# Pass two's offset convolution: nine taps in three column groups of the PE array, added up by a selecting matmul at the turn

## The chip, the cores and the metric

The kernel runs on one core of one Trainium2 chip. The time is the device time of one execution in microseconds. The engines are TensorE (PE, with its weight loads as PEld), VectorE (DVE), ScalarE (ACT), GpSimd (POOL), which here only issues gathers, and SyncE (SP), which issues plain DMAs.

## What is computed

The input is 32 images of 96 channels and 48 x 48 pixels. Two layers run one after the other. The first is a state space mixer and a quantised feed-forward net; the second, which the change touches, is a deformable convolution and another feed-forward net:

```python
offset = _conv(x, offset_w, offset_b)           # 3x3, 96 -> 18 channels
mask = jax.nn.sigmoid(_conv(x, mask_w, mask_b)) # 3x3, 96 -> 9 channels
for k in range(K * K):
    i, j = (k // K, k % K)
    py = base_y[None, :, None] + i * DIL + offset[:, 2 * k]
    px = base_x[None, None, :] + j * DIL + offset[:, 2 * k + 1]
    samp = _bilinear(x, py, px) * mask[:, k][:, None]
    out = out + jnp.einsum('bchw,oc->bohw', samp, weight[:, :, i, j])
```

The two small convolutions are done as one, with 27 output channels and nine taps: the offset convolution.

## The kernel before

Pass one (up to 13.4 ms of the trace) does the scans of the first layer and is not touched. Pass two takes the images in a software pipeline: one call of `pass_two`, a stage, finishes image d (called D) while it prepares image c (called C). There are 33 stages: the first has only C, the last only D, and 31 have both. Between two stages stand barriers and the clearing of the semaphores.

An image is cut into six chunks of 384 pixels (CH), and a chunk into three tiles of 128. A stage runs seven periods p = 0 to 6 of twelve steps u = 0 to 11. Each engine has its program written out over these steps, and the order of the code is the order of the work:

- C's half, chunk c = p: the out projection (L1487, u = 1), its first feed-forward net (L1441, L1448, L1458, L1465), the norm that gives `xflat` and `xn`, the turn of `xflat` (L1497) and the rows `prow`, which SP stores to the corner table (L1381). Then comes the offset convolution of chunk q (L1516). For q = 0 to 3 it stands in period q + 2, steps 6 to 8; for q = 4 in period 6, steps 2 to 4; for q = 5 in period 6, steps 7 to 9. Its step `stage` does taps 3·stage to 3·stage + 2, all into partitions 0 to 26 of PSUM bank BM. One step later ACT adds the bias and writes `offc` (L1630), and one more step later PE turns `offc` by three transposes (L1531) and ACT splits the result into `offs` and `sig` (L1636, L1637).
- When all of C's chunks are through, DVE works out the positions and weights of all samples (`positions`, L1347 to L1366), which the gathers of the next stage need.
- D's half: POOL issues 162 indirect gathers (L1404), nine for each of 18 tiles t, into a ring G of four tiles. DVE multiplies a tile by its weights in two halves (L1680), PE turns the 36 blocks (L1420, 16 + 16 + 4), ACT copies them to `cols_t` (L1569), and once a chunk PE convolves (L1434, step 3 of the next period). Tile 3p + u // 4 is multiplied in period p at steps where u % 4 is 0 or 1, and turned one tile later. Then come the norm of chunk e (L1441 at step 6, L1448 at step 7, DVE's L1690 at step 8) and the second feed-forward net (L1458 at steps 9 and 10, L1465 at step 0 of the next period).
- SP loads the inputs of the next C after C's last rows are stored (L1388 to L1390) and stores D's output when its last chunk is done (L1394).

Of one engine's program everything waits behind a waiting instruction. All matmuls named here but L1458 and L1465 (fp8) are fp32.

Of the kernel before, what the change touches and what calls it, by code (L numbers as in the profile page):

```python
# [17 lines left out]
CH = 8 * W  # L18
# [16 lines left out]
def shape_constants():  # L35

    c = {}
    c["ident"] = np.eye(P, dtype=np.float32)
    c["centring"] = (np.eye(C) - 1.0 / C).astype(np.float32)
    c["mean"] = np.full((C, C), 1.0 / C, np.float32)  # L40
    c["ones"] = np.ones((P, P), np.float32)
    j, i = np.meshgrid(np.arange(P), np.arange(P), indexing="ij")
    c["before"] = (j < i).astype(np.float32)
    r = np.arange(C)
    state = np.repeat(np.arange(N).reshape(NG, NG), GS, axis=1)
    c["pick"] = (r[:, None, None] % (2 * N) == state[None]).astype(np.float32).reshape(C, NG * P)
    c["sel"] = (np.arange(P)[:, None, None] % GS + GS * np.arange(CG)[None, :, None] == r[None, None, :]).astype(
        np.float32).reshape(P, CG * C)
    c["shifts"] = np.concatenate([(r[:, None] == r[None, :] + k - 2).astype(np.float32) for k in range(5)], axis=1)
    px = np.arange(P)[:, None, None] + P * np.arange(NT)[None, :, None]  # L50
    tap = np.arange(TAPS)[None, None, :]
    c["base_y"] = (px // W - 1 + tap // 3).astype(np.float32).reshape(P, NT * TAPS)
    c["base_x"] = (px % W - 1 + tap % 3).astype(np.float32).reshape(P, NT * TAPS)
    c["border"] = np.ones((1, PH, PW), np.float32)
    c["border"][:, 0] = c["border"][:, -1] = 0
    c["border"][:, :, 0] = c["border"][:, :, -1] = 0
    c["border"] = c["border"].reshape(1, PH * PW)
    return c
# [11 lines left out]
def build_program(nc, I, out, B=IMAGES):  # L70

    with ExitStack() as top:
# [56 lines left out]
        off_b = cols[0:3 * TAPS, 50:51]  # L129
# [206 lines left out]
        with ExitStack() as loop:  # L336
            M = pass_two_memory(sbt, loop)
            w_def = sbt(loop, "w_def", [C, TAPS, C])
            w_off = sbt(loop, "w_off", [C, TAPS, 3 * TAPS])
# [11 lines left out]
            with ExitStack() as ctx:  # L351
                Z = sems(top, "z_set", "z_done")
                zero_rows = sbt(ctx, "zero_rows", [PH, CORNERS * C])
                with nc.Block() as block:
                    @block.vector
                    def _(dve):
                        dve.memset(zero_rows[:], 0.0).then_inc(Z["z_set"], 1)
                        dve.memset(M["xn"][:, 0:PH:PH - 1, :], 0.0)
                        dve.memset(M["xn"][:, 1:PH - 1, 0:PW:PW - 1], 0.0)

                    @block.sync
                    def _(sp):
                        sp.wait_ge(Z["z_set"], 1)
                        for table in tables:
# [5 lines left out]
                        sp.dma_start(flat(w_off), I["w_off"]).then_inc(Z["z_done"], 16)  # L370
                        sp.wait_ge(Z["z_done"], 16 * (2 * PH + 4))
# [4 lines left out]
                           w_off=w_off, off_b=off_b, w_def=w_def)  # L376
# [898 lines left out]
def pass_two_memory(sbt, ctx):  # L1275
# [4 lines left out]
        offc=b("offc", [3 * TAPS, CH]), prow=b("prow", [PT, 2, ROWT, C]), offs=b("offs", [P, NT, 3 * TAPS]),  # L1280
# [10 lines left out]
def pass_two(nc, ps, S, M, Wt, dram, parity, d_image, c_image, load):  # L1291
# [76 lines left out]
    with nc.Block() as block:  # L1368
# [42 lines left out]
        def _(pe):  # L1411
# [57 lines left out]
            for p, u in places:  # L1469
# [36 lines left out]
                if q is not None and stage < 3:  # L1506
# [8 lines left out]
                    for k in range(3 * stage, 3 * stage + 3):  # L1515
                        m = pe.matmul(ps[0:3 * TAPS, BM, 0:CH], Wt["w_off"][:, k, :],  # L1516
                                      M["xn"][:, 8 * q + k // 3:8 * q + k // 3 + 8, k % 3:k % 3 + W],
                                      start=(k == 0), stop=(k == TAPS - 1))
                    if stage == 2:
                        m.then_inc(S["p_off"], 1)  # L1520
                if q is not None and stage == 4:
# [8 lines left out]
                    for r in range(TILES):  # L1530
                        m = pe.transpose(ps[:, BN, 3 * TAPS * r:3 * TAPS * (r + 1)], M["offc"][:, r * P:(r + 1) * P],  # L1531
                                         ident[0:3 * TAPS, 0:3 * TAPS])
# [26 lines left out]
        def _(act):  # L1559
# [42 lines left out]
            for p, u in places:  # L1602
# [25 lines left out]
                if q is not None and stage == 3:  # L1628
                    act.wait_ge(S["p_off"], q + 1)
                    act.activation(M["offc"][:], ps[0:3 * TAPS, BM, 0:CH], ACT.Identity,  # L1630
                                   bias=Wt["off_b"]).then_inc(S["p_offs"], 1)
# [172 lines left out]
```

## Time and profile before

| | us |
|---|---|
| median of 3 runs | 22115.79 |
| lowest and highest | 22111.92 to 22125.49 |
| the profiled execution | 22081.76 |
| its span, first to last instruction | 22079.9 |
| mean granted TensorE clock over the span | 0.832 |

The profile is of one execution. Times of rows are microseconds from the start of the span, durations of one instruction are nanoseconds. A matmul's recorded duration holds its way through the array, so matmuls in a row overlap in the records: what one of them takes of the engine's time is the distance between their starts. A row of the timeline can hold several instructions of one line: "x6" are six.

### The profile page before, as it was taken

The page shows a single profiled execution, that of the slowest core. Times are in us where ns is not written, and L with a number is a line of the kernel's source. Part 1 is how long each engine was busy: PE and PEld are TensorE (multiplying, and loading weights), DVE is VectorE, ACT ScalarE, POOL GpSimd, SP SyncE. Part 2 cuts the span into 40 slices and gives each one's busy share as a digit, 9 for nine tenths or more (in the row PEclk, how much of TensorE's full clock was granted, in tenths as well). Part 3 has the DMA queues.
Part 4 walks back from the last instruction along what each step waited for, and adds up shares of the span by engine and source line. Part 5 has one row for each costly group of instructions (what it writes and reads, how often), then busy time and mean ns, then how long its engine had stood idle before and what let it go on. Part 6 is the DMA issues. An engine that isn't in the chain of part 4 may idle for free. (4 is left out here: it accounts for less than half of the span.)

```text
span 22079.9 us, 218895 instructions
## 1 busy us (share of the span) xinstructions
PE 15826.8 (72%) x70927; PEld 8399.6 (38%) x70927; DVE 13815.1 (63%) x14097; ACT 8761.1 (40%) x15494; POOL 11403.5 (52%) x9476
## 2 busy tenths in 40 slices
PE   6677677676676676676676665777777777777777
PEld 3233233233333333333333332444444444444444
DVE  5778778778777787777787782444444444444443
ACT  3344343343443443443443432333333333333332
POOL 3454454454454444444454453555555555555555
PEclk8788788788787787787787787988898888989898
DMA  2222222232222322322322223555555555555554
GB/s 56 71 78 73 73 77 70 76 77 68 77 77 67 78 75 68 79 73 69 79 74 69 77 78 98 148 145 147 146 149 147 148 145 146 149 147 148 146 145 133
DMA packets 1287149, 2235.23 MB, mean 101 GB/s; under 512 B 710836, under 2 KB 754216, under 8 KB 1270504
## 3 DMA queue, kind: packets, MB, share of 16 engines
q1 hardware_dynamic: 874248, 1086.64, 19.1%
q0 software_dynamic: 368640, 1076.24, 17.2%
q10 hardware_dynamic: 43008, 56.65, 0.9%
q8 instruction: 663, 10.86, 0.2%
q14 instruction: 590, 4.83, 0.1%
HBM read 1493.57 MB, written 271.92 MB: 80 GB/s over the span
## 5 line engine op out<-in xcount | busy, mean ns | idle before, releaser
L1250 POOL TENSOR_TENSOR hc<-h,crep 128x768 f32<-128x768 f32 x2304 | 4172.2, 1812 | 5950.1 <-DVE h L1029 3900.9
L1404 POOL DMA_INDIRECT G<-corners,idx x5184 | 4929.6, 951 | 3831.8 <-issue 2494.3
L646 PE MATMUL ps<-hc,sel 128*96 128x512 f32 (+1 forms) x9216 | 4080.7, 572 | 541.7 <-POOL hc L1250 337.3
L1680 DVE TENSOR_TENSOR G<-G,ps 128x1536 f32<-128x1536 f32 (+1 forms) x1152 | 2235.4, 1946 | 1890.0 <-DMA G<-corners,idx 1889.5
L1029 DVE TENSOR_TENSOR_SCAN h<-decay,carry,ps 128x768 f32<-128x768 f32 x1536 | 2774.9, 1807 | 79.0 <-ACT decay L841 19.6
L1420 PE MATMUL ps<-ident,G 128*96 128x128 f32 x20736 | 2716.7, 285 | 38.4 <-DVE G L1680 38.4
L1013 DVE TENSOR_TENSOR ps<-dxr,ps 128x768 f32<-128x768 f32 x2304 | 2180.7, 946 | 862.2 <-PE ps L635 833.5
L1420 PEld LDWEIGHTS ps<-ident,G 128*96 128x96 f32 x20736 | 2473.2, 133 | 390.3 <-issue 296.0
L646 PEld LDWEIGHTS ps<-hc,sel 128*96 128x96 f32 x9216 | 1600.1, 189 | 2543.5 <-issue 1920.2
L635 PE MATMUL ps<-bq,pick 96*128 96x512 bf16 (+1 forms) x4608 | 1298.9, 368 | 1654.0 <-DVE h L1029 1592.3
L841 ACT ACTIVATE decay<-dtr,a_neg 128x768 f32<-128x768 f32 x2304 | 2125.6, 928 | 780.8 <-DVE h L1029 710.1
L849 ACT ACTIVATE carry<-h 128x1 f32<-128x1 f32 x1536 | 308.9, 201 | 3833.5 <-DVE h L1029 3829.1
L715 PE MATMUL ps<-xcp,w_local 96*96 96x384 f32 x3456 | 1424.7, 533 | 252.8 <-ACT local_c L907 252.0
L1029 DVE TENSOR_TENSOR_SCAN h<-decay,ps 128x768 f32<-128x768 f32 x768 | 1340.2, 1745 | 21.7
L1516 PE MATMUL ps<-xn,w_off 96*27 96x384 f32 x3456 | 1288.7, 515 | 10.1 <-ACT xn L1614 10.1
L1569 ACT ACTIVATE cols_t<-ps 96x512 f32<-96x512 f32 (+1 forms) x1728 | 827.1, 481 | 1157.5 <-PE ps L1420 1157.1
L635 PEld LDWEIGHTS ps<-bq,pick 96*128 96x128 bf16 x4608 | 363.3, 101 | 2422.2 <-DVE h L1029 1749.4
L1434 PE MATMUL ps<-cols_t,w_def 96*96 96x384 f32 x3456 | 1156.3, 489 | 142.4 <-ACT prow L1620 140.0
L674 PE MATMUL ps<-xnp,w_conv 97*96 97x384 f32 x3456 | 1180.8, 486 | 42.7 <-ACT eout L932 39.2
L1575 ACT ACTIVATE sq<-ps 96x384 f32<-96x384 f32 x576 | 280.1, 486 | 2302.5 <-PE ps L1441 2299.7
L1690 DVE TENSOR_TENSOR xq<-ps,rs 96x384 fp8e5<-96x384 f32 x384 | 212.0, 552 | 1453.9 <-ACT rs L1583 1453.7
L715 PEld LDWEIGHTS ps<-xcp,w_local 96*96 96x96 f32 x3456 | 612.8, 184 | 722.8 <-ACT local_c L907 324.6
(214 smaller groups left out, 21501.1 us busy)
## 6 DMA issues: line engine op xcount, KB each, us to landing
crep<-c_rows SPq DMA_DIRECT2D x3072, 96.0 KB, 2.3
dtr<-rel SPq DMA_DIRECT2D x2304, 96.0 KB, 2.2
dxr<-mag SPq DMA_DIRECT2D x2304, 96.0 KB, 2.2
corners<-prow SPq DMA_DIRECT2D x1536, 72.0 KB
G<-corners,idx POOLq DMA_INDIRECT x5184
x_in<-in_x SPq DMA_DIRECT2D x32, 864.0 KB
local_all<-local_c ACTq DMA_DIRECT2D x192, 144.0 KB, 1.9
unit<-sorted_rows SPq DMA_DIRECT2D x32, 864.0 KB, 6.8
```

The costliest lines, as they stand in the source:

```text
L635: m = pe.matmul(wide(bank_of(("step", s)), P)[:, a:b], Wt["pick"][:, ng, :], bq[:, q % 2, a:b], start=True, stop=True)
L646: m = pe.matmul(wide(BY, C)[:, a:b], Wt["sel"][:, cg, :], hc[:, v % HC, a:b], start=(v % ROUND == 0), stop=(v % ROUND == ROUND - 1))
L674: m = pe.matmul(ps[0:C, BS + c % 2, 0:CH], Wt["w_conv"][:, t, :], xn[0:C + 1, 8 * c + t // 3:8 * c + t // 3 + 8, t % 3:t % 3 + W], start=( ...
L715: m = pe.matmul(ps[0:C, BV, 0:CH], Wt["w_local"][:, t, :], xpad[:, 8 * c + t // 3:8 * c + t // 3 + 8, t % 3:t % 3 + W], start=(t == 0), st ...
L841: act.activation(decay[:, s % 3, :], dtr[:, q % 2, cg, :], ACT.Exp, scale=Wt["a_neg"][:, direction(q)[0], ng, cg:cg + 1]).then_inc(S["s_de ...
L1013: dve.tensor_tensor(drive, dxr[:, q % 2, cg, :], drive, ALU.mult).then_inc(S["s_drive"], 1)
L1029: dve.tensor_tensor_scan(along(h[:, v % 3, :], k), along(decay[:, v % 3, :], k), along(wide(bank_of(("step", v)), P), k), first, ALU.mult, ...
L1250: pool.tensor_tensor(hc[:, s % HC, :], h[:, s % 3, :], crep[:, g % CRING, :], ALU.mult).then_inc(S["s_weighted"], 1)
L1404: pool.indirect_dma_start(M["G"][:, t % GRING, k, :], None, table_d, bass.IndirectOffsetOnAxis(M["idx"][:, t, k:k + 1], 0)).then_inc(S[f"p ...
L1420: m = pe.matmul(ps[0:C, BT + n % 2, (k % 4) * P:(k % 4 + 1) * P], M["G"][:, v % GRING, k, q * C:(q + 1) * C], ident[:], is_transpose=True, ...
L1516: m = pe.matmul(ps[0:3 * TAPS, BM, 0:CH], Wt["w_off"][:, k, :], M["xn"][:, 8 * q + k // 3:8 * q + k // 3 + 8, k % 3:k % 3 + W], start=(k = ...
L1680: dve.tensor_tensor(g, g, w.to_broadcast([P, (k1 - k0) * CORNERS, C]), ALU.mult).then_inc(S["p_prod"], 1)
```

## The change

The array is split by columns. The nine taps go to three column groups of 32 columns, one for each row i of the 3 x 3 taps; the group i writes its sum over its three taps to partitions 32·i to 32·i + 31 of the same bank. Step `stage` of the convolution now does the taps 3·i + stage of all three groups, one after the other. The three partial sums are not added there: the copy to `offc` takes all 96 partitions (the bias on the first group only), and the turn is now an ordinary matmul with `offc` as the stationary operand and a 96 x 27 matrix `sel_off` of zeros and ones as the moving one, which picks channel o from the three groups and so adds them. The weights `w_off` are padded from 27 to 32 columns, with zeros set by DVE before pass two, and three small loads join that setup.

```diff
@@ constants
+    c["sel_off"] = (r[:, None] % GS == np.arange(3 * TAPS)[None, :]).astype(np.float32)
@@ setup of pass two
-            w_off = sbt(loop, "w_off", [C, TAPS, 3 * TAPS])
+            w_off = sbt(loop, "w_off", [C, TAPS, GS])
+            off_bias = sbt(loop, "off_bias", [C, 1])
+            sel_off = sbt(loop, "sel_off", [C, 3 * TAPS])
...
+                        dve.memset(w_off[:], 0.0).then_inc(Z["z_set"], 1)
+                        dve.memset(off_bias[:], 0.0).then_inc(Z["z_set"], 1)
...
-                        sp.dma_start(flat(w_off), I["w_off"]).then_inc(Z["z_done"], 16)
+                        sp.dma_start(w_off[:, :, 0:3 * TAPS],
+                                     I["w_off"].rearrange("c (k o) -> c k o", o=3 * TAPS)).then_inc(Z["z_done"], 16)
+                        sp.dma_start(off_bias[0:3 * TAPS], I["cols"][0:3 * TAPS, 50:51],
+                                     allow_slow_non_contiguous=True).then_inc(Z["z_done"], 16)
+                        sp.dma_start(sel_off[:], I["sel_off"]).then_inc(Z["z_done"], 16)
@@ pass_two_memory
-        offc=b("offc", [3 * TAPS, CH]), prow=b("prow", [PT, 2, ROWT, C]), offs=b("offs", [P, NT, 3 * TAPS]),
+        offc=b("offc", [C, CH]), prow=b("prow", [PT, 2, ROWT, C]), offs=b("offs", [P, NT, 3 * TAPS]),
@@ pass_two, tensor
-                    for k in range(3 * stage, 3 * stage + 3):
-                        m = pe.matmul(ps[0:3 * TAPS, BM, 0:CH], Wt["w_off"][:, k, :],
-                                      M["xn"][:, 8 * q + k // 3:8 * q + k // 3 + 8, k % 3:k % 3 + W],
-                                      start=(k == 0), stop=(k == TAPS - 1))
+                    for i in range(3):
+                        m = pe.matmul(ps[GS * i:GS * (i + 1), BM, 0:CH], Wt["w_off"][:, 3 * i + stage, :],
+                                      M["xn"][:, 8 * q + i:8 * q + i + 8, stage:stage + W],
+                                      start=(stage == 0), stop=(stage == 2))
...
-                        m = pe.transpose(ps[:, BN, 3 * TAPS * r:3 * TAPS * (r + 1)], M["offc"][:, r * P:(r + 1) * P],
-                                         ident[0:3 * TAPS, 0:3 * TAPS])
+                        m = pe.matmul(ps[:, BN, 3 * TAPS * r:3 * TAPS * (r + 1)], M["offc"][:, r * P:(r + 1) * P],
+                                      Wt["sel_off"][:], start=True, stop=True)
@@ pass_two, scalar
-                    act.activation(M["offc"][:], ps[0:3 * TAPS, BM, 0:CH], ACT.Identity,
-                                   bias=Wt["off_b"]).then_inc(S["p_offs"], 1)
+                    act.activation(M["offc"][:], ps[0:C, BM, 0:CH], ACT.Identity,
+                                   bias=Wt["off_bias"][:]).then_inc(S["p_offs"], 1)
```

The places in the engines' programs stay. This is PE's program from the last turn of samples to the end of a stage, before:

```order
L1516 MATMUL ps<-xn,w_off 27x384 x3
L1434 MATMUL ps<-cols_t,w_def 96x384 x9
L1516 MATMUL ps<-xn,w_off 27x384 x6
L1531 MATMUL ps<-ident,offc 128x27 x3
L1441 MATMUL ps<-x,centring 96x384
```

And the same place in the changed kernel, whose lines are eight further down:

```order
L1524 MATMUL ps<-xn,w_off 32x384 x3
L1442 MATMUL ps<-cols_t,w_def 96x384 x9
L1524 MATMUL ps<-xn,w_off 32x384 x6
L1539 MATMUL ps<-sel_off,offc 128x27 x3
L1449 MATMUL ps<-x,centring 96x384
```

No instruction moved past another. The column groups, which these rows don't show, are in the partitions that the convolution writes.

## Rows read from the trace of the kernel before

**Rows 1.** The page's parts 1 and 2: busy shares; 40 slices of the span

```profile
PE 15826.8 (72%) x70927; PEld 8399.6 (38%) x70927; DVE 13815.1 (63%) x14097; ACT 8761.1 (40%) x15494; POOL 11403.5 (52%) x9476
PE   6677677676676676676676665777777777777777
PEclk8788788788787787787787787988898888989898
```

**Rows 2.** Timeline of POOL (start us, duration us, gathers, idle before): starts and last gathers of stages

```profile
13566.73 0.94 POOL L1404 DMA_INDIRECT G<-corners,idx  x1 [285.24 <-POOLq L160]
13768.74 0.95 POOL L1404 DMA_INDIRECT G<-corners,idx  x1 [0.30 <-issue]
...
15372.85 1.05 POOL L1404 DMA_INDIRECT G<-corners,idx  x1 [0.30 <-issue]
15431.16 0.94 POOL L1404 DMA_INDIRECT G<-corners,idx  x1 [57.26 <-POOLq L160]
...
21840.62 0.94 POOL L1404 DMA_INDIRECT G<-corners,idx  x1 [59.71 <-POOLq L160]
```

**Rows 3.** Timeline of PE: projections of two periods in a row, and the tail's begin

```profile
15321.48 0.81 PE L1487 MATMUL ps<-mix,wg 96*96 96x384 f32 x2
15356.45 0.81 PE L1487 MATMUL ps<-mix,wg 96*96 96x384 f32 x2
15371.11 2.12 PE L1516 MATMUL ps<-xn,w_off 96*27 96x384 f32 x6
15373.16 0.89 PE L1441 MATMUL ps<-x,centring 96*96 96x384 f32 x2
15384.84 0.81 PE L1441 MATMUL ps<-x,centring 96*96 96x384 f32 x2
15394.61 6.05 PE L1434 MATMUL ps<-cols_t,w_def 96*96 96x384 f32 x18
15400.59 4.05 PE L1516 MATMUL ps<-xn,w_off 96*27 96x384 f32 x12
15405.31 0.36 PE L1531 MATMUL ps<-ident,offc 27*128 27x27 f32 x3 [0.66 <-ACT offc L1630]
15406.10 0.86 PE L1441 MATMUL ps<-x,centring 96*96 96x384 f32 x2 [0.43 <-issue]
15406.89 2.12 PE L1516 MATMUL ps<-xn,w_off 96*27 96x384 f32 x6
15408.94 0.89 PE L1448 MATMUL ps<-sq,mean 96*96 96x384 f32 x2
15409.76 4.05 PE L1516 MATMUL ps<-xn,w_off 96*27 96x384 f32 x12
```

**Rows 4.** Timeline of DVE in the same stage, and tile 17 of the first stage

```profile
15366.41 1.75 DVE L1680 TENSOR_TENSOR G<-G,ps 128x1536 f32<-128x1536 f32 x1 [6.07 <-DMA G<-corners,idx]
15378.58 1.74 DVE L1680 TENSOR_TENSOR G<-G,ps 128x1536 f32<-128x1536 f32 x1
13784.05 1.74 DVE L1680 TENSOR_TENSOR G<-G,ps 128x1536 f32<-128x1536 f32 x1
```

**Rows 5.** Timeline of PEld: weight loads around the offset convolution

```profile
15064.78 0.16 PEld L1441 LDWEIGHTS ps<-x_t,centring 96*96 96x96 f32 x1 [0.16 <-issue]
...
15400.59 0.13 PEld L1516 LDWEIGHTS ps<-xn,w_off 96*27 96x27 f32 x2 [0.57 <-issue]
15400.93 0.10 PEld L1516 LDWEIGHTS ps<-xn,w_off 96*27 96x27 f32 x1 [0.22 <-issue]
15401.26 0.10 PEld L1516 LDWEIGHTS ps<-xn,w_off 96*27 96x27 f32 x1 [0.22 <-issue]
```

**Rows 6.** All instructions of the turn L1531: durations ns min/median/max

```profile
L1531 PEld LDWEIGHTS ps<-ident,offc x576: 132/136/139, 13456.6 to 21824.6; 27*128 27x128 f32 x192
```

**Rows 7.** Timeline of ACT in the tail: square after norm 3, and the chain's inverse

```profile
15407.00 0.49 ACT L1575 ACTIVATE sq<-ps 96x384 f32<-96x384 f32 x1 [0.99 <-PE ps L1441]
15410.47 0.52 ACT L1583 ACTIVATE rs<-rs 96x384 f32<-96x384 f32 x1
```

More of the change, by code:

```diff
@@ L128, in build_program @@
         local_w = cols[:, 40:49]
-        off_b = cols[0:3 * TAPS, 50:51]
         def clear(own, dma_sems):
@@ L362, in _ @@
                     def _(sp):
-                        sp.wait_ge(Z["z_set"], 1)
+                        sp.wait_ge(Z["z_set"], 3)
                         for table in tables:
@@ L369, in _ @@
                         sp.dma_start(flat(w_def), I["w_def"]).then_inc(Z["z_done"], 16)
-                        sp.dma_start(flat(w_off), I["w_off"]).then_inc(Z["z_done"], 16)
-                        sp.wait_ge(Z["z_done"], 16 * (2 * PH + 4))
+                        sp.dma_start(w_off[:, :, 0:3 * TAPS],
[3 more added lines that the diff above has]
+                        sp.dma_start(sel_off[:], I["sel_off"]).then_inc(Z["z_done"], 16)
+                        sp.wait_ge(Z["z_done"], 16 * (2 * PH + 6))
                 nc.all_engine_barrier()
@@ L375, in build_program @@
                            bn_scale=bn_scale, bn_shift=bn_shift, col=col, w1q=w1q, w2q=w2q, b1q=b1q, b2q=b2q,
-                           w_off=w_off, off_b=off_b, w_def=w_def)
+                           w_off=w_off, off_bias=off_bias, sel_off=sel_off, w_def=w_def)
             dram = dict(x=I["x"], local=local_dram, mamba=mamba_dram, tables=tables, out=out)
```

## The prediction

> **What bounds the kernel now.** The page's busy shares and slices come first [rows 1]. Pass two is the last 15 or 16 of the 40 slices, where PE stands at 7 tenths and its clock mostly at 8 and 9 tenths of full speed. That looks like a PE bound, with a convolution of 3456 matmul instructions worth cutting. The second view corrects this: the timeline of POOL. A stage's 162 gathers follow one another without a pause, 202.01 us from the first to the last in the first such stage (13566.73 to 13768.74) and 201.69 in the shown middle one, which is 1.25 us for each [rows 2]. Only 31 gaps between stages interrupt POOL. From the first gather of all to the first gather of the last stage are 21840.62 - 13566.73 = 8273.9 us in 31 stages, 266.9 each. So a stage with both halves costs 202.2 us of gathers that nothing on PE can shorten, and 64.7 us from the last gather to the next stage's first. Only these 64.7 can shrink, 2006 us in all.
>
> Third view, PE against POOL. Two projections of neighbouring periods lie 34.97 us apart [rows 3], while 27 gathers take 33.75. PE is the slower one by 1.2 us a period, so it falls behind and pays for it after the last gather. DVE's rows show how far [rows 4]: tile 16 was waited for (6.07 us idle, released by the DMA at 15366.41), so tile 17 could start nine gathers or 11.25 us later, at 15377.66, which is 4.8 us after the last gather. It started at 15378.58, 5.7 us after it. In the first stage it started 15.3 us after (13784.05 against 13768.74). Over the 31 stages, of which these two are near the ends, this distance is 5.6 to 15.7 us, 9.2 in the mean. The last chunk's convolution (L1434) starts 21.8 us after the last gather in the shown stage and 25.4 in the mean.
>
> Then comes the tail: convolution, norm 3, variance, feed-forward, positions, barriers. In the shown stage it takes 15431.16 - 15394.61 = 36.6 us, in the mean of 31 stages 39.3, and 25.4 + 39.3 = 64.7. PE has two offset convolutions in it, between steps of that very chain [rows 3].
>
> **What one step of the convolution costs.** Three taps are "x6": every fp32 matmul is two instructions in a row, each with its weight load. A call from L1516 to L1441 takes 15373.16 - 15371.11 = 2.05 us. Inside a call the loads lie 0.32 us apart and last 0.10, so PE is bound by the stream of the moving operand [rows 5]. Six times 0.32 is 1.94, and 0.11 is left at the edges. There the next line's load isn't pulled ahead: the load at 15400.59 comes with its matmul, after 0.57 us of idle, whereas 15064.78 comes a full slot before its own [rows 5]. The 27-column matmul already runs in another division of the array than its neighbours. That toll is paid now and stays.
>
> **What column groups do to it.** No row shows two groups at work together, so the saving is bounded. Call r the saving of one call of six, R that of twelve in a row (tail, 15400.59).
>
> - Upper end: all three groups stream together, and a call is two slots instead of six. r = 4 x 0.32 = 1.29, R = 2.58.
> - Lower end: no overlap, r = 0, or less than that if each change of group costs an edge (the rival below).
> - What I take: the two instructions of one matmul follow each other in the same group, so the second must wait for the first, and what starts in order behind it waits too. Second half of A goes with first half of B, second half of B with first of C. A call is four slots, r = 2 x 0.32 = 0.65, and twelve are seven, R = 1.61. If the load of a new group (0.10) can only begin when the matmul ahead has started, two of these come on top: r = 0.44, R = 1.09. I take the middle, r = 0.54 and R = 1.35, because the loads in [rows 5] start with the matmul ahead, while a group that this matmul doesn't use might be loaded sooner.
>
> The page "TensorE: Matmul & The Clock Gate" of the Trainium skill (Part 3) says that matmuls in different tiles overlap but start and end strictly in program order, which is the in-order start assumed here. The same part gives 2.38 times for three column tiles of 512 columns; by that a call would take 2.05 / 2.38 = 0.86 us, near the 0.76 of the first rival below.
>
> **The turn.** Three transposes become three ordinary fp32 matmuls, so six instructions, and each loads 128 columns (0.136 us, [rows 6]). The nearest rows bound it: three transposes take 0.36 now, and three more loads at 0.06 to 0.14 add 0.18 to 0.42. I take 0.4. The copy to `offc` is 384 elements per partition as before, on 96 partitions instead of 27; this costs nothing on an engine that works all partitions at once (0.57 us on 27, 0.52 for the 96-partition copy L1583 of the same width [rows 7]). The setup (two memsets, three loads) happens once, some us beside about a hundred row loads: nothing.
>
> **The sum for a stage with both halves.** First, PE's lag. Periods 2 to 5 have one convolution each: 4 x (3 x 0.54 - 0.4) = 4.9 us. The call at step 2 of period 6, ahead of L1434, adds 0.54, so 5.4. But the gathers set a floor. DVE can't multiply tile 17 before 4.8 us after the last gather, then comes the residual behind it (0.9), which L1441 (15384.84) waits for: 4.8 + 1.7 + 0.9 = 7.4 instead of 12.0 us after the last gather, so in the shown stage at most 4.6 + 0.54 are won. Stages with more lag get all 5.4. Mean of 31: 5.3.
>
> Second, the tail. Twelve instructions stand before the turn that norm 3 waits behind: 1.35 - 0.4. The six before L1448 at 15408.94: the square is ready at 15407.00 + 0.49, so up to 1.4 of r can be had: 0.54. The twelve before the feed-forward (15409.76): the inverse is ready at 15410.99 and DVE's multiply at 15411.6, PE at 15413.7, so up to 2.1: 1.35. The last turn has idle time of PE beside it. Sum 2.84.
>
> Together 8.1 us, times 31 = 252. The first stage has no gathers and is all chain: six convolutions of 18 instructions each save some 2 us, 12. That is 264 of 22081.8 in the profiled execution. This execution is 34 us under the median of the runs, so the saving is taken off the median: 22115.8 - 264 = 21852, rounded to **21850**.
>
> **The rivals.**
>
> *All three groups at once* (r = 1.29, R = 2.58). For: the array's columns are separate. Against: the pairs in one group. PE would save 4 x 3.5 = 14 us before the tail, and nearly every stage would run into the gathers' floor: convolution 16.0 us after the last gather instead of 25.4, so 9.4. Tail: 2.58 - 0.4 + 1.29 + 2.1 = 5.6. Together 15.0 x 31 = 465, and 21 in the first stage: **21630**.
>
> *No overlap.* The groups run one after the other, and the turns alone are added: 4 x 0.4 + 0.4 = 2.0 us a stage, 31 stages and 2 more: 64 at most, 30 with 0.18 for a turn: **22150 to 22180**. For it: no row shows overlap. The change then doesn't do what it says.
>
> *A toll at each change of group* is the case on the other side. If the array treats a new group as it treats the edge between L1516 and its neighbours, the load comes late and about 0.1 us is lost. Each call has two changes, twelve instructions five, and nothing overlaps. Periods 2 to 5: 4 x (6 x 0.1 + 0.4) = 4.0; the tail 14 x 0.1 + 0.4 = 1.8; 5.8 x 31 + 7 = 187: **22300**. With both sides of the edge counted at each change (0.11 before, 0.16 at the first matmul after, 0.89 against 0.81 in [rows 3]) it is 22500. It decides from the point where the tolls of a call exceed the overlap. Against: all nine taps are in the same division of the array.
>
> *PE gets faster but its clock falls.* The slices of the clock show 8 and 9 tenths [rows 1]; PE with more idle time could be granted 1.2 instead of 2.4 GHz more often. A slow spell doubles every slot. Eight us a stage would have to be eaten; within 0.2% of no change.
>
> **How the numbers follow.** Pairwise overlap 0.50, all three at once 0.15, no overlap 0.14, a toll 0.14, the clock 0.07. The toll, 22300 and above, is left out of the range, which spans the others with the bounds of the turn: 21620 to 22190. The likeliest case alone spans r from 0.44 to 0.65: 21800 to 21920. A measurement of this kernel can tell about 0.2%, 44 us, from no change. Faster by more than that: pairwise and all three, 0.65. Slower: toll, and half of no overlap, 0.21. Within: 0.14.
>
> **What would show it.** In the changed profile the call of six should take 1.4 to 1.6 us from its start to the next line's, not 2.05 (0.8 is the first rival, 2.05 the second, more the third); the call of twelve 3.2 to 3.7 from L1524 to the copy's release, less than 4.05; the recorded matmuls of two groups should start closer than 0.32. POOL's gathers must still take 202 us a stage. The gap between stages should shrink from 64.7 to 56.6, and tile 17 should be multiplied about 5 us after the last gather in most stages. The forecast is wrong if the groups don't overlap, if the stages' lag comes from spells of slow clock and not from PE's work, or if POOL begins to wait for PE.

## The result

| | us |
|---|---|
| before, median of 4 runs beside it | 22113.85 (22106.08 to 22125.49) |
| after, median of 4 runs | 21616.36 (21604.64 to 21625.43) |
| ratio | 0.9776, 95% interval 0.9763 to 0.9788 |
| the profiled execution of after, its span | 21612.28, 21610.5 |
| forecast | 21850, range 21620 to 22190 |

The changed kernel is 2.2% faster. The direction was right, the gain was nearly twice the forecast, and the time lies 4 us under the range. The first rival, all three groups at once, gave 21630.

One thing is needed to read the experiments. Eleven of the eighteen kernels ran on chips on which the kernel before takes 23,960 to 24,000 us. Its spans of pass two look different there (last section). Each ratio is against runs of the kernel before on the same chip, and the two settings are kept apart below.

### The profile page after: what moved, and what is told of

Read it like the earlier page. It is cut to its first block and busy times, and to the rows that moved or that the text cites. A ratio compares the mean times of both kernels' runs of the same rounds, so it can differ in the third digit from the quotient of the medians.

```text
span 21610.5 us, 220051 instructions
## 1 busy us (share of the span) xinstructions
PE 15250.9 (71%) x71503; PEld 8297.3 (38%) x71503; DVE 13802.1 (64%) x14099; ACT 8777.7 (41%) x15494; POOL 11400.7 (53%) x9476
## 3 DMA queue, kind: packets, MB, share of 16 engines
q0 software_dynamic: 368640, 1076.24, 17.6%
## 5 line engine op out<-in xcount | busy, mean ns | idle before, releaser
L1412 POOL DMA_INDIRECT G<-corners,idx x5184 | 4925.0, 950 | 3357.5 <-issue 2263.5
L1688 DVE TENSOR_TENSOR G<-G,ps 128x1536 f32<-128x1536 f32 (+1 forms) x1152 | 2237.2, 1947 | 2343.1 <-DMA G<-corners,idx 2343.1
L1442 PE MATMUL ps<-cols_t,w_def 96*96 96x384 f32 x3456 | 1156.3, 489 | 141.5 <-ACT prow L1628 139.0
L1118 DVE TENSOR_SCALAR cmp<-sim,dist 128x128 bf16<-128x128 f32 (+8 forms) x576 | 854.1, 1483 | 6.3 <-ACT sim L908 3.6
L1442 PEld LDWEIGHTS ps<-cols_t,w_def 96*96 96x96 f32 x3456 | 547.7, 163 | 686.9 <-issue 489.9
```

The lines of the kernel that those rows point to most:

```text
L1412: pool.indirect_dma_start(M["G"][:, t % GRING, k, :], None, table_d, bass.IndirectOffsetOnAxis(M["idx"][:, t, k:k + 1], 0)).then_inc(S[f"p ...
L1442: m = pe.matmul(ps[0:C, BN, 0:CH], Wt["w_def"][:, k, :], M["cols"][:, e % 2, k, :], start=(k == 0), stop=(k == TAPS - 1))
L1688: dve.tensor_tensor(g, g, w.to_broadcast([P, (k1 - k0) * CORNERS, C]), ALU.mult).then_inc(S["p_prod"], 1)
```

## The profile of the changed kernel

Lines are eight further down than before: L1524 is the offset convolution, L1539 its turn, L1412 the gather, L1688 the multiply, L1442 the convolution of samples. In twogroups, groupcall and aab the offset convolution is L1525, in normfirst its turn is L1545.

First the page's second part: PE's busy share, and the granted clock in 40 slices (answers to [rows 1]).

```profile
PE   6677677667667767767767764777777777777776
PEclk8788788778778878878878876888888888888888
```

But for the last slice, PE is as busy in pass two as before, in tenths. Part of that can come from the clock. Added up from the clock intervals after 13500 us, PE was at 1.2 GHz for 1910 of 8580 us before and for 2093 of 8110 us after.

POOL's timeline (answers to [rows 2]): the first gather of all, one stage's first and last gather, the next stage's first, and the first of the last stage.

```profile
13559.70 0.94 POOL L1412 DMA_INDIRECT G<-corners,idx  x1 [269.29 <-POOLq L160]
...
15071.18 0.94 POOL L1412 DMA_INDIRECT G<-corners,idx  x1 [51.99 <-issue]
...
15273.85 0.94 POOL L1412 DMA_INDIRECT G<-corners,idx  x1 [0.30 <-issue]
15321.38 0.94 POOL L1412 DMA_INDIRECT G<-corners,idx  x1 [46.59 <-POOLq L160]
...
21370.28 0.94 POOL L1412 DMA_INDIRECT G<-corners,idx  x1 [46.91 <-POOLq L160]
```

The gathers of a stage still take 202.7 us. The gain is in the gap behind them, 47.5 us here and 49.9 in the mean of 31, where it was 64.7. Over 31 stages a stage takes (21370.28 - 13559.70) / 31 = 251.95 us instead of 266.9. That is 14.95 x 31 = 463 us. The spans of the two profiled executions differ by 469 us, and the 7 us more lie ahead of the first gather (although pass one ended 9 us later in this execution, so the first stage gained some 16). The other 28 of the 498 us between the medians are no gain of a place in the kernel: the profiled execution before was 32 us under its median, the one after 4 us.

PE's timeline in the tail of that stage (answers to [rows 3]):

```profile
15289.26 0.85 PE L1524 MATMUL ps<-xn,w_off 96*32 96x384 f32 x6 [0.33 <-ACT xn L1622]
15290.03 6.05 PE L1442 MATMUL ps<-cols_t,w_def 96*96 96x384 f32 x18
15296.01 1.49 PE L1524 MATMUL ps<-xn,w_off 96*32 96x384 f32 x12
15298.19 0.85 PE L1539 MATMUL ps<-sel_off,offc 96*128 96x27 f32 x6 [0.69 <-ACT offc L1638]
15299.48 0.86 PE L1449 MATMUL ps<-x,centring 96*96 96x384 f32 x2 [0.43 <-issue]
15300.26 0.85 PE L1524 MATMUL ps<-xn,w_off 96*32 96x384 f32 x6
15301.04 0.89 PE L1456 MATMUL ps<-sq,mean 96*96 96x384 f32 x2
15301.85 1.49 PE L1524 MATMUL ps<-xn,w_off 96*32 96x384 f32 x12
15303.74 0.50 PE L1466 MATMUL ps<-xq,w1q 96*128 96x384 fp8e5 x2 [0.39 <-DVE xq L1698]
```

A call is 15290.03 - 15289.26 = 0.77 us instead of 2.05, twelve instructions are a row of 1.49 instead of 4.05. The weight loads agree (answers to [rows 5]; columns as there):

```profile
15296.01 0.15 PEld L1524 LDWEIGHTS ps<-xn,w_off 96*32 96x32 f32 x6 [0.57 <-issue]
15296.36 0.12 PEld L1524 LDWEIGHTS ps<-xn,w_off 96*32 96x32 f32 x3 [0.20 <-issue]
15296.68 0.12 PEld L1524 LDWEIGHTS ps<-xn,w_off 96*32 96x32 f32 x3 [0.20 <-issue]
```

Where before one load followed each 0.32 us, three stand in one row per slot. The toll of the line's edge (0.57 us idle of PEld) has stayed.

Last, DVE's tile 17 of the same stage (answers to [rows 4]), 2.96 us after the last gather's start at 15273.85:

```profile
15276.81 1.75 DVE L1688 TENSOR_TENSOR G<-G,ps 128x1536 f32<-128x1536 f32 x1 [1.94 <-DMA G<-corners,idx]
```

It waits for the DMA. In all 31 stages it starts 2.95 to 3.26 us after the last gather, 3.05 in the mean (before 9.2), and in 29 of them the profile names the DMA as what released it. The list of waits of 14000 to 20000 us says the same of all tiles, before first and after second (us in total, times, longest):

```profile
DVE G L1680 <- DMA G<-corners,idx: 1284.6, 235, 12.3
```

```profile
DVE G L1688 <- DMA G<-corners,idx: 1726.8, 384, 12.4
```

## The experiments

The question after the result was why three groups overlap fully, though the two halves of a float32 matmul follow each other in one group. The theory: a waiting second half doesn't hold up what stands behind it. PE starts a later instruction of another group. The rival: the gain isn't from overlap but from something that came with the change (padded weights, the wider copy, setup). A second question was whether the stage's time follows PE's by the path sum.

**onegroup**, all nine taps in one group again, with everything else of the change kept:

```diff
-                    for i in range(3):
-                        m = pe.matmul(ps[GS * i:GS * (i + 1), BM, 0:CH], Wt["w_off"][:, 3 * i + stage, :],
...
+                    for k in range(3 * stage, 3 * stage + 3):
+                        m = pe.matmul(ps[0:GS, BM, 0:CH], Wt["w_off"][:, k, :],
...
```

The lines left out take the taps in their old order and let `sel_off` read the first group alone.

> The changed kernel with all nine taps in column group 0 (32 columns, in the old order of the taps); copy, turn and setup stay changed. Theory (the whole gain is the overlap of the groups): a call of six takes 2.05 us again, and what is left is the dearer turn. The changed kernel's turn takes 0.69 us from its start to the next line's, against 0.30 before, so 0.39 x 5 = 2.0 us a stage on PE's path, x 31 = 60: about 22175 us, 1.0028 of before. Rival A (part of the gain comes from the copy, the padding or the turn): under 22070. Rival B (the turn is hidden in PE's waits for ACT): 22115, as before.

> The one-group kernel once more, beside the two above on the same chip: where the kernel before takes 22114, 22175 (the turns' 2.0 us a stage); where it takes 24000, 24120, as in its first run. If the clock is what differs between the two settings, its share of 1.2 GHz is that of the kernel before within 0.02.

> Theory (PE's time is what the gap follows, and only a different column group lets PE start a later instruction): all nine taps in one group give calls of 2.05 us again and leave only the longer turn, so 0 to 2 us a stage more than before, ratio 1.000 to 1.003. Where POOL's gathers take 202 us a stage this should be read in the gap: 64.7 to 66.7 us. Rival (the padded weights, the copy of 96 partitions or the setup brought the gain): 0.978, the gap 50 us.

Where before takes 23,960 to 24,000: 1.0054 (1.0037 to 1.0071) and 1.0005 (0.9995 to 1.0014), 23973.31 us in the second run, where 24120 had been expected. Where it takes 22,120.11: 22212.42 us, 1.0042 (1.0025 to 1.0059). The gain is gone, so the groups made it and not the rest. Timeline of PE in onegroup_third, a call and the turn:

```profile
15128.94 2.12 PE L1524 MATMUL ps<-xn,w_off 96*32 96x384 f32 x6
15130.99 0.89 PE L1449 MATMUL ps<-x,centring 96*96 96x384 f32 x2
...
15142.06 0.85 PE L1539 MATMUL ps<-sel_off,offc 96*128 96x27 f32 x6 [0.55 <-ACT offc L1638]
```

A call is 2.05 us again. What is left is the turn's price, expected at up to 2 us a stage and a gap of 66.7 us; the stage came out 3.5 us longer (270.38), with a gap of 68.0. The rest isn't explained; PE was at 1.2 GHz for 121 us more than in the kernel before, which at half speed can be up to 60 of the 92 us.

**twogroups**, the nine taps alternating between two groups:

```diff
+                    for k in range(3 * stage, 3 * stage + 3):
+                        i = k % 2
+                        m = pe.matmul(ps[GS * i:GS * (i + 1), BM, 0:CH], Wt["w_off"][:, k, :],
...
```

> The changed kernel with two column groups instead of three, the taps going to them in turn: a call is A B A or B A B. Every theory gives four slots a call, r = 0.65, which is the saving that the forecast took for three groups at its better end; the twelve of the tail take six or seven slots. So this run tests the forecast's sum with its own r made real. Sum with the floor as the changed trace shows it (convolution 16.2 us after the last gather): lag 6.7 us a stage, tail 3.9, together 10.6 x 31 + 12 = 340: 21775 us, 0.9846 of before. By the forecast's own numbers (lag 5.3 to 6.3, tail 2.8 to 3.5) 21800 to 21850. If the sum was wrong in its path and not only in r, the time lies outside 21740 to 21850.

> The two-group kernel once more, on the same chip as the two above. Where the kernel before takes 22114: 21775, the sum of its first run. Where it takes 24000: 23980, as in its first run, and a share of 1.2 GHz above that of the one-group kernel by 0.04, which is the rival of the run before this one (the clock gives the gain back).

> Theory (a group runs beside the others, a call lasts as long as its longest group): a call is four slots, 1.41 us where 0.77 and 2.05 stand in the other two, twelve in a row are six slots, 2.1 us. By the same path sum: 4 x (3 x 0.6 - 0.4) + 0.6 = 6.2 us of lag and 1.95 - 0.4 + 0.6 + 1.95 = 4.1 us of tail, 10 us a stage, 325 us: ratio 0.985, if POOL's gathers take 202 us a stage. Rival (the gap has a floor that two groups already reach): 0.978 as with three. Rival (where the program before takes about 23980, gaps and gathers both change and the sum does not hold): 0.994 to 0.999 as measured twice.

0.9991 (0.9981 to 1.0001) and 0.9945 (0.9928 to 0.9961) where before takes 23,960 to 24,000; 21762.3 us, 0.9839 (0.9823 to 0.9856) where it takes 22,120. Timeline of PE there (twogroups_third):

```profile
14427.88 1.48 PE L1525 MATMUL ps<-xn,w_off 96*32 96x384 f32 x6
14429.38 0.86 PE L1449 MATMUL ps<-x,centring 96*96 96x384 f32 x2
...
14556.72 2.13 PE L1525 MATMUL ps<-xn,w_off 96*32 96x384 f32 x12
```

Calls of 1.41 to 1.50 us and twelve in 2.13: as long as the fuller group. The stage takes 256.81 us, 10.1 less than before; 10 was expected. So the path sum came out here, once it was given the right length of a call. On the other chips it didn't: the same kernel won nothing in its first run and 0.6% in its second, where 23,980 had been expected and 23829.96 came.

**groupcall**, each call does all three taps of one group:

```diff
+                    i = stage
+                    for j in range(3):
+                        m = pe.matmul(ps[GS * i:GS * (i + 1), BM, 0:CH], Wt["w_off"][:, 3 * i + j, :],
...
```

> The changed kernel, but step s of the convolution does the three taps of group s, so that the six instructions of a call are all in one group, and only the twelve in a row of the tail have six of one group followed by six of another. It asks how far ahead PE looks past an instruction that waits for its group. Theory 1 (each group has a deep queue of its own): the twelve take about six slots, 2.05 us instead of 3.9, twice a stage: 3.6 us won, 2.0 lost on the turns, about 22065 us. Theory 2 (PE only passes a waiting instruction by a few places): the six of the second group start one or two slots before the first group's last, the twelve take 3.3 to 3.9 us, and the time is that of the one-group kernel or up to 35 us less, 22140 to 22175.

24054.86 us, 1.0022 (1.0012 to 1.0032), beside 24123.6 for onegroup on the same chip. Its timeline of PE:

```profile
14513.55 2.12 PE L1525 MATMUL ps<-xn,w_off 96*32 96x384 f32 x6 [0.32 <-ACT xn L1623]
...
14521.58 2.80 PE L1525 MATMUL ps<-xn,w_off 96*32 96x384 f32 x12
```

A call alone has one group and takes its 2.05. But twelve in a row, A A A A A A B B B B B B, take 2.80 and not 4.05, which lies between the two theories (2.05, and 3.3 to 3.9) and fits neither. These are the recorded starts in us behind the first, here and in the changed kernel. The records don't name the group; in onegroup, where all are of one group, two starts are never closer than 0.32, so starts that lie closer belong to different groups.

```
groupcall  x12  0  .347  .670 .676  .992 1.023  1.317 1.346  1.639 1.668  1.991  2.313
changed    x12  0  .006  .013  .348 .354 .360  .670 .679 .683  .993 1.000 1.005
changed    x6   0  .006  .013  .347 .354 .361
```

B's first starts at 0.676, with A's third at 0.670, while A's fourth to sixth still wait. It didn't start with A's first or second, and so it is in all 46 twelves of this trace that ran at 2.4 GHz. The rule that fits: PE looks past three waiting instructions and no more, so an instruction starts if its group is free and it is at most four places behind the running one. In the changed kernel's order A A B B C C this reaches C's first half at once. By the same rule a look-ahead of one or two places would have given the forecast's four slots a call, and one of three places three slots. Whether the limit counts matmuls, as here, or weight loads or both together, these runs don't tell.

**aab** tests that rule by an order that it had not seen, two taps of A and then one of B in each call (shown against twogroups; the marks of a group's first and last tap follow):

```diff
-                        i = k % 2
+                        i = k % 3 // 2
```

> Two groups, and in every call two taps of group A and then one of group B (six instructions A A A A B B). The rule read from groupcall is that PE starts an instruction of another group once it is within four places behind the running one. By it B's first half starts beside A's first (under 0.02 us after it), B's second at 0.35, and a call is four slots, 1.41 to 1.49 us. With three places B's first half would start at 0.35, with two at 0.67, in order at 1.32 and the call would be five or six slots (1.7 to 2.05).

```
aab        x6   0  .014  .347 .361  .670  .993
aab        x12  0  .014  .348 .361  .670  .993  1.318 1.324  1.640 1.671  1.961  2.284
```

```profile
15004.96 1.48 PE L1525 MATMUL ps<-xn,w_off 96*32 96x384 f32 x6
15006.45 0.86 PE L1449 MATMUL ps<-x,centring 96*96 96x384 f32 x2
```

B's first half, four places behind A's, started 0.014 us after it, as the rule says. In the twelve, B's third (place 11) starts with A's fifth (place 7, at 1.318) and not before, which the rule says too.

A call is 1.41 to 1.50 us, the four slots of the forecast's main case, so this kernel is also that case made real: one run of 21921.1 beside 22111.58, a stage of 261.38 us. Here the path sum fails: 5.5 us a stage came, less than the forecast's 8.1. The lag paid what the sum says (the last convolution starts 19.0 us after the last gather instead of 25.4, 6.4 against 5.3 to 6.3), the tail nothing (39.9 us instead of 39.3, where a gain of 2.8 was forecast). Up to norm 3 the tail is 0.8 us shorter (11.5 to 10.7), behind it 1.4 longer, and there PE was at 1.2 GHz for 26.8 us a stage instead of 17.6. At half speed that is up to 4.6 us, enough for the missing 3.4; that it is the cause isn't shown.

**threetaps** asks whether PE's lag is used up:

```diff
-                    for i in range(3):
+                    for i in range(3 if q >= 4 or stage == 0 else 0):
...
```

This kernel leaves out six of the nine taps for chunks 0 to 3, so its offsets are others.

> The changed kernel without the second and third step of the offset convolution for chunks 0 to 3 (six of nine taps left out, so offsets are others); chunks 4 and 5 keep all nine. PE has 4 x 1.54 = 6.2 us less to do in each stage, all of it while the gathers run. Theory (after the change the gathers set the pace, and the last tile comes through as early as it can): no more than 0.6 us a stage, 21595 to 21616 us. Rival (PE still sets the pace of part of the stages): up to 6.2 x 31 = 190 us less, 21425.

> It leaves out the second and third step of the offset convolution for chunks 0 to 3 (six of their nine taps), so 1.5 us less of PE in each of periods 2 to 5. Theory (with three groups tile 17 already waits for its gather and not for PE): the gap stays where the changed kernel has it, within 1 us of 50, ratio 0.976 to 0.979. Rival (PE's lag still counts): 6 us a stage less, 0.969.

0.9878 (0.9861 to 0.9894) where before takes 24,000. Where it takes 22,120: 21679.36 us, 0.9799 (0.9783 to 0.9815). Leaving out 1.5 us of PE in each of four periods brought nothing: the gap is 51.6 us instead of 49.9, a little over the 1 us that was allowed for, and the time is 40 to 63 us above the changed kernel's. The multiply of tile 17 is at its floor in both (3.18 and 3.05 us). So the lag was used up with three groups. That it got slower fits the forecast's last rival: PE was at 1.2 GHz for 2510 us of pass two, 417 more than in the changed kernel, in 231 spells instead of 149, and at half speed that can cost more than the 63.

**normfirst** asks whether the tail is paid in full. Norm 3 of the last chunk is issued ahead of the last turn of the offsets, which gets another bank; the waits and the ACT copies follow:

```diff
+                if u == 6 and e is not None and p == NCH:
+                    if d is not None:
+                        pe.wait_ge(S["p_row"], d + 1)
+                        pe.wait_ge(S["p_osplit"], NCH - 2)
+                    norm("3", "p_x3", e + 1, M["x3"][:, part(e)], BN)
...
-                        m = pe.matmul(ps[:, BN, 3 * TAPS * r:3 * TAPS * (r + 1)], M["offc"][:, r * P:(r + 1) * P],
+                        m = pe.matmul(ps[:, BT if p == NCH else BN, 3 * TAPS * r:3 * TAPS * (r + 1)], M["offc"][:, r * P:(r + 1) * P],
...
```

> An improvement of the changed kernel. In the tail PE's norm 3 stands behind the turn of chunk 4's offsets and shares its bank; now norm 3 and its square stand ahead of that turn, and the turns of chunks 4 and 5 use a bank of the samples, which is free by then. In the changed trace norm 3 starts at 15299.48 though its input is ready at 15296.7 and the convolution's twelve instructions are through at about 15297.2. Theory (norm 3 is on the chain that ends the stage): 2.1 us a stage, 65 us, about 21550 us. Rival (the chain then waits for the offsets of chunk 5 or for ACT's copy): 21600 to 21616.

> The changed kernel with norm 3 of the last chunk issued ahead of the last turn of the offsets. Theory (in the tail every us on PE between the last convolution and the barrier is paid): norm 3 starts 2.0 us earlier, the turn's copies follow it, so 1 to 2 us a stage, 30 to 62 us: ratio 0.975 to 0.9765 against 0.9776 of the changed kernel. Rival (the turn of the offsets and the positions behind it end last, not the norm's chain): no gain or a loss, 0.9776 or above.

> The changed kernel itself, beside the next one in the same comparison: 0.9776 where the kernel before takes about 22,115; 0.9856 where it takes 23,960.

> The changed kernel with norm 3 of the last chunk ahead of the last turn of the offsets. Theory (the tail is paid in full): 1 to 2 us a stage, 30 to 62 us under the changed kernel, ratio 0.9745 to 0.9765 where the kernel before takes about 22,115. Rival (the two differ by chips and not by the order): the same ratio as the changed kernel within 0.1%.

Side by side (after_third, normfirst_fourth): the changed kernel 21639.37 us, 0.9785 (0.9771 to 0.9798); with the earlier norm 21560.55 us, 0.9747 (0.9733 to 0.976). On another chip (normfirst_third) it was 21561.47, 0.9746 (0.973 to 0.9763). The five times of each don't overlap (21621.49 to 21656.50 against 21542.62 to 21561.53). Timeline of PE in normfirst_third:

```profile
15279.44 1.49 PE L1524 MATMUL ps<-xn,w_off 96*32 96x384 f32 x12
15280.86 0.89 PE L1449 MATMUL ps<-x,centring 96*96 96x384 f32 x2
15281.62 0.85 PE L1545 MATMUL ps<-sel_off,offc 96*128 96x27 f32 x6
```

Norm 3 starts 1.42 us after the twelve begin, against 15299.48 - 15296.01 = 3.47 in the changed kernel: 2.05 us earlier. The stage is 252.57 - 250.07 = 2.5 us shorter (79 us over 31 stages, the difference of the medians). That is what the tail's being paid in full asks for, and this kernel beats both. One thing beside the order has changed: behind the start of norm 3, PE was at 1.2 GHz for 16.3 us a stage against 21.9 in after_third, which can be worth up to 2.8 us. So the size of what the order alone gives isn't shown. On the other chips nothing was to be seen: 0.9868 (0.9851 to 0.9884) on chip 10 against 0.9856 for the changed kernel on chip 14.

**eight_before** and **eight_after** take the ninth gather of every sample tile out of either kernel, to see whether POOL's gathers set the stage's length on those other chips:

```diff
-                    for k in range(TAPS):
+                    for k in range(TAPS - 1):
...
```

> The kernel before with eight of the nine gathers of each tile (the ninth sample of every pixel is left out, its place in the ring holds zeros). POOL has 18 x 1.25 = 22.5 us less to do in a stage, 30.0 us a period instead of 33.75. Theory (before the change PE, at 34.97 us a period, sets the pace once it has caught up with the gathers): only the start of a stage gains, 1 to 5 us a stage, 21960 to 22085 us. Rival (the gathers set the pace): 22.5 x 31 = 700 us less, 21415.

> The changed kernel with eight of the nine gathers of each tile, as in the run on the kernel before. Theory (after the change the gathers at 33.75 us a period set the pace, while PE needs 34.97 - 3 x 1.28 + 0.39 = 31.5): the time falls until PE is the bound again, 10 to 18 us a stage, so to 21060 to 21310 us. Rival (PE or the chain through the engines is the bound in both kernels): as little as on the kernel before, 1 to 5 us a stage, 21460 to 21585.

23409.91 beside 23982.95 us, 0.9763 (0.9746 to 0.9779), and 22983.09, 0.9585 (0.9569 to 0.9601). 18 gathers of 1.25 us are 22.5 us a stage or 720 over 32. Measured were 573 on the kernel before. A stage got 17.5 us shorter (308.20 against 325.67 of before_again) and 20.1 on the changed one (295.22 against 315.28). Both expectations, 1 to 5 and 10 to 18 us, missed; they were made for the chips where the gathers take 202 us. The stretch of gathers went from 244.4 us only to 227.0 on the kernel before. So there the gathers aren't issued without a pause: POOL waits inside a stage, as this row of before_again shows:

```profile
13649.20 0.95 POOL L1404 DMA_INDIRECT G<-corners,idx  x1 [4.08 <-PE ps L1420]
```

**before_again** and **after_again** are the two kernels themselves on such a chip:

> The kernel before, unchanged, for its own profile beside the experiments' comparison, where its median was 24000 us and not 22114. Theory (PE's clock): in those comparisons PE was granted 1.2 GHz for 0.34 to 0.45 of pass two against 0.22 in the profile of the kernel before; if this run is at 24000 again, it shows at least 0.34 too, and POOL waits for PE inside the stages, which it never does at 22114. If it is back at 22114, its share is 0.22. Rival (slower gathers or memory): the share is 0.22 at 24000, and the gathers land later than 2.7 us after their issue.

> The changed kernel, unchanged, beside the kernel before. Theory (three groups take 1.28 us off each call at 2.4 GHz and twice that at 1.2 GHz, and only PE's work and the gathers' pace decide): where the kernel before takes 22114, this takes 21616, ratio 0.978; where it takes 24000 PE is the bound throughout, the gathers leave room, so the gain per stage is 5 x 3.84 - 2 = 17 us or more: 23400 us or less, 0.975 or less. Rival (the clock gives part of it back: PE with less work is granted 1.2 GHz more often): at 24000 the ratio is between 0.98 and 0.995, and the share of 1.2 GHz is above that of the kernel before.

23960.79 us, 1.0001 (0.9991 to 1.001), and 23618.05, 0.9856 (0.984 to 0.9873). The change gains 1.4% there instead of 2.2%. A stage goes from 325.67 to 315.28 us, all of it in the gap (81.3 to 70.7); the gathers take 244 us in both. PE's time at 1.2 GHz in pass two rises from 3876 to 4361 us.

Of before_again's two explanations the clock's sign came (a share of 0.37, at least 0.34 was asked for) and the memory's didn't: where DVE waits for a gather there (tiles 0 and 1), it is released 2.95 to 3.14 us after the tile's last gather, as in the kernel before (2.92 to 3.14). The clock alone isn't enough: 62 us a stage more at 1.2 GHz are worth up to 31 of the 58.8 us by which the stage is longer. The last section shows what else is different.

Of after_again's two, "23400 us or less" failed and its rival came: the ratio lies between 0.98 and 0.995, with a higher share of 1.2 GHz (0.43). The same goes for twogroups_again, whose share (0.42) lies 0.04 above onegroup_again's, as expected. The tail gives the same as on the other chips (38.3 to 33.1 us). What is missing is in the lag: the last convolution starts 5.3 us earlier after the last gather and not 9.4, and while the gathers run PE is at 1.2 GHz for 114.9 us a stage instead of 96.3, worth up to 9 us.

## Why the forecast was off

**Where the gain falls** was right: POOL's gathers stayed at 202 us, what the 31 stages gained came out of the gap, and POOL hardly waits for PE inside a stage (14 us in all of pass two).

**The failing step** is "the second must wait for the first, and what starts in order behind it waits too". The first half of that sentence is right: second halves start 0.32 to 0.35 after the first. The second half is wrong. PE passes over up to three waiting instructions, so for PE the sentence ahead of the forecast, that everything waits behind a waiting instruction, is wrong too. A call is two slots of 0.32 and an edge of 0.13, r = 1.28 instead of 0.54, R = 2.56 instead of 1.35. The rule of the page "TensorE: Matmul & The Clock Gate" of the Trainium skill (Part 3), starts strictly in program order, doesn't hold across column groups here: the first halves of B and C start 0.34 us ahead of the second half of A that stands before them. Its 2.38 times for three column tiles of 512 columns lies below the 2.05 / 0.77 = 2.66 measured here with 384.

**The turn** was right: 15246.42 - 15245.73 = 0.69 us from L1539's start to the next line's, against 0.30 for the transposes, so 0.4 more.

```profile
15245.73 0.85 PE L1539 MATMUL ps<-sel_off,offc 96*128 96x27 f32 x6 [0.55 <-ACT offc L1638]
15246.42 0.48 PE L1466 MATMUL ps<-xq,w1q 96*128 96x384 fp8e5 x2
```

**The floor** of tile 17, 4.8 us after the last gather, was read too high. It came from tile 16, whose gathers lay beside the row stores (15358.79 to 15362.22). It is 3.0.

**The sum** of the first rival was then right almost to the microsecond: convolution 9.4 us earlier (25.43 to 16.07 us after the last gather), tail 5.6 expected and 39.3 - 33.9 = 5.4 measured, 465 us expected over 31 stages and 463 measured. Part of this is luck. With the forecast's floor the norm behind the last residual starts 7.4 us after the last gather and the convolution 15394.61 - 15384.84 - 1.29 = 8.5 us later, which makes its 16. In the shown stage of the changed kernel this norm starts at

```profile
15280.24 0.81 PE L1449 MATMUL ps<-x,centring 96*96 96x384 f32 x2
```

which is 6.4 us after the last gather, and the convolution follows 9.8 us later, with PE at 1.2 GHz in between (granted clock 0.59 from 15282.6 to 15286). The floor was too high and the clock was left out, by about as much. The same sum gave 10 us for two groups, and 10.1 came; for aab it gave too much. The setup, the copy to `offc` and the padding cost nothing that onegroup shows apart from the turn, unless it is in the 1.5 us a stage that stayed unexplained there.

**The chances.** I had a published price beside the page's own rule (2.38 against strict order), and for matmuls that come in pairs the two don't fit together: with strict order six instructions take four slots, which is 1.5 times. The page doesn't say whether its figure is for pairs, so this alone decided nothing, but it was a reason to give the rival at 21630 more than the 0.15 that it got for the one argument "pairs in one group".

**The toll** didn't come: PE pays nothing for a change of group, 0.007 us between starts. **The clock** may have come, as a part: PE is at 1.2 GHz a larger share of pass two in every kernel that has less for PE to do. The 183 us more in the changed kernel are worth up to 92 us; how much of the gain they took back isn't shown.

## What to carry to other kernels

If a chain of small matmuls writes few output columns, split it by column groups and issue the groups in turn, so that each next group stands at most four places behind; all of one group first loses part of it (twelve in a row: 2.80 us, against 2.13 with two groups in turn) or, within a call of one group, all of it. Read the gain from the engine that issues the work (here the gap of POOL), not from PE's busy share. When the lag is gone, more relief of PE bought nothing here, and the next microseconds were in the tail.

## What the runs showed of the hardware

**A look-ahead of four places** between column groups on PE, from the starts above: four places behind is started (changed kernel, aab), five is not (groupcall).

**Late releases behind PE.** On chips 3, 10 and 14, where the kernel before takes some 24,000 us, pass one takes the same time as elsewhere, and pass two 22% more. The timeline of before_again shows what is different. First the kernel before on the first chip, then on such a one:

```profile
15319.74 1.91 PE L1420 MATMUL ps<-ident,G 128*96 128x128 f32 x16
15321.68 0.59 ACT L1569 ACTIVATE cols_t<-ps 96x512 f32<-96x512 f32 x1 [1.26 <-PE ps L1420]
```

```profile
13637.78 2.35 PE L1420 MATMUL ps<-ident,G 128*96 128x128 f32 x20
13639.97 0.81 PE L1487 MATMUL ps<-mix,wg 96*96 96x384 f32 x2
13640.61 0.49 PE L1497 MATMUL ps<-ident,xflat 96*96 96x96 f32 x4
13647.12 0.59 ACT L1569 ACTIVATE cols_t<-ps 96x512 f32<-96x512 f32 x1 [10.14 <-remote]
13648.01 0.61 DVE L1731 SCALAR_TENSOR_TENSOR x_t<-ps,cols,x_t 96x384 f32<-96x384 f32 x1 [6.24 <-remote]
```

In the first the copy starts as soon as the transposes are recorded as ended. In the second ACT and DVE are idle until 7 us after PE's records, and both are let go within a microsecond. Taking every copy L1569 for which ACT was idle: in the kernel before it starts 0.04 us after the recorded end of the matmul in all 999 cases, and it is so in the changed kernel and in those of chips 6 and 8. In before_again half of 934 are later than 1.2 us, a tenth later than 8.7, the longest 29.6, at the same places of each stage. Whether PE itself stands still there or only its signals are late, the records don't tell; they show no work on PE in the gap. Why three chips do so and the others don't stays open. There POOL waits for PE inside a stage, and the same change gives 1.4%.

**The clock and less work.** In pass two PE was at 1.2 GHz for 1910 us before, 2093 with three groups, 2510 with part of the taps left out (threetaps). Only the last step is clear: a second trace of the changed kernel (after_third) has 2178, and onegroup, in which PE has no less to do than before, has 2031. In slices of the whole span that is hardly to be seen, in the sum of the intervals it is.
